# Three expert tiles issued in quarters inside the attention score blocks

## The reference, cut to what matters

```python
x = layernorm(x + L0_attn(x))   # linear attention over L2-normalised Q, K
x = layernorm(x + L0_ffn(x))    # 8 experts, all computed, weighted
x = layernorm(x + L1_attn(x))   # attention between the 16 heads of a token
x = layernorm(x + L1_ffn(x))    # router, top 75% of tokens, gelu(x @ w)
```

```python
# L0_ffn
gate = softmax(x @ gate_w + gate_b)
w = gate * (gate >= 0.1); w = w / sum(w)
out = sum over e of w[:, e] * (x @ expert_w[e] + expert_b[e])     # e = 0..7
# L1_attn
scores = einsum('bnhd,bngd->bnhg', q, k) / 8     # 16 x 16 per token
attn = softmax(scores)
out = einsum('bnhg,bngd->bnhd', attn, v)
```

## Time and profile before

| | |
|---|---|
| median of three runs | 1433.84 us |
| the profiled execution | 1434.45 us, span 1432.6 us |
| PE busy | 84% of the span |
| DVE busy | 64% |
| ACT busy | 51% |
| POOL busy | 40% |
| mean granted TensorE clock | 0.855 of full speed |

### The profile page before, as it was taken

How to read it: one execution, slowest core, us unless ns; L and a number is a source line. 1 busy time by engine, 2 the same in 40 slices (tenths; PEclk the granted TensorE clock), 3 DMA queues, 4 the chain that set the end, 5 groups by cost and what they waited for, 6 DMA issues and landing times.

```text
span 1432.6 us, 31148 instructions
## 1 busy us (share of the span) xinstructions
PE 1202.3 (84%) x12264; PEld 760.1 (53%) x12264; DVE 915.9 (64%) x2113; ACT 733.3 (51%) x1156; POOL 570.2 (40%) x887
## 2 busy tenths in 40 slices
PE   6689899997999899988999899988999898784443
PEld 3444456654665556654665556654665545442442
DVE  3534666587677866587677866587677776464534
ACT  3222465347554765357554675357454675356423
POOL 3125326425424525435424525435524515331312
PEclk8579998899879988899879987899879987787566
DMA  5000090205411190206410290207420290209220
GB/s 177 15 1 15 30 161 4 75 15 148 60 32 45 70 152 3 75 16 148 60 46 31 86 136 2 75 16 154 54 60 2 79 128 2 59 16 168 24 60 30
DMA packets 93145, 90.64 MB, mean 63 GB/s; under 512 B 7110, under 2 KB 81864, under 8 KB 92744
## 3 DMA queue, kind: packets, MB, share of 16 engines
q1 hardware_dynamic: 81736, 76.06, 26.8%
q0 software_dynamic: 2560, 8.39, 1.7%
q10 hardware_dynamic: 8704, 4.20, 1.1%
HBM read 46.68 MB, written 41.94 MB: 62 GB/s over the span
## 4 chain that ended last, share of the span: by engine, by line
PE 53%; DVE 18%; POOL 7%; issue 7%; DMA 6%; ACT 6%; SPq 2%; ACTq 1%; POOLq 0%; DVEq 0%
PE bank L1512 50%; DVE keys L1296 3%; POOL rs L521 2%; DVE x L1201 2%; DVE gelu L1298 2%; DVE stats L1060 2%; ACT x L793 1%; PE bank L1522 1%; DMA scratch_qkv<-part 1%; DMA scratch_qkv<-stage 1%; DMA bt<-scratch_o 1%; DVE ct L1030 1%; DMA scratch_o<-stage 1%; POOL stage L572 1%; DMA ct<-scratch_qkv 1%
## 5 line engine op out<-in xcount | busy, mean ns | idle before, releaser
L1512 PE MATMUL bank<-we,at 128*128 128x512 f16 x1536 | 365.5, 399 | 0.0
L1512 PEld LDWEIGHTS bank<-we,at 128*128 128x128 f16 x1536 | 154.0, 102 | 191.9 <-issue 36.4
L536 POOL TENSOR_TENSOR part<-part 128x512 f32<-128x512 f32 x64 | 83.0, 1297 | 353.8 <-ACTq L819 353.8
L671 ACT ACTIVATE part<-bank,wexp 128x256 f32<-128x256 f32 x256 | 105.2, 471 | 185.7 <-PE bank L1512 124.2
L1201 DVE SCALAR_TENSOR_TENSOR x<-bank,wexp,x 128x256 f32<-128x256 f32 x256 | 122.9, 480 | 81.0 <-PE bank L1512 75.0
L1512 PE MATMUL bank<-bt,wqkv 128*128 128x512 f16 x576 | 139.7, 385 | 15.6 <-DVE stage L1030 12.9
L793 ACT ACTIVATE x<-x,nm,rs 128x256 f32<-128x256 f32 x192 | 104.6, 593 | 92.5 <-POOL nm L524 91.2
L517 POOL TENSOR_SCALAR nm<-mv 128x2 f32<-128x2 f32 x128 | 32.3, 252 | 254.0 <-DVE mv L1065 248.5
L1030 DVE TENSOR_TENSOR stage<-bank,stage 128x512 f16<-128x512 f32 x112 | 75.6, 686 | 85.3 <-ACT stage L671 85.0
L1512 PE MATMUL bank<-keys,blockdiag 128*128 128x16 f16 x3072 | 96.6, 193 | 24.3 <-DMA keys<-scratch_qkv 18.5
L1512 PEld LDWEIGHTS bank<-keys,blockdiag 128*128 128x128 f16 x3072 | 95.6, 104 | 29.5 <-DMA keys<-scratch_qkv 19.0
(11 more groups left out here) (176 smaller groups left out, 2268.8 us busy)
## 6 DMA issues: line engine op xcount, KB each, us to landing
scratch_qkv<-stage SPq DMA_DIRECT2D x40, 512.0 KB, 3.8
ct<-scratch_qkv SPq DMA_DIRECT2D x128, 128.0 KB, 5.7
x_in<-in_x_dram SPq DMA_DIRECT2D x32, 256.0 KB, 2.7
keys<-scratch_qkv SPq DMA_DIRECT2D x64, 128.0 KB, 5.1
bt<-scratch_o SPq DMA_DIRECT2D x16, 512.0 KB, 3.7
out_dram<-x POOLq DMA_DIRECT2D x32, 256.0 KB, 2.7
scratch_qkv<-part SPq DMA_DIRECT2D x8, 512.0 KB, 8.2
scratch_o<-stage SPq DMA_DIRECT2D x32, 128.0 KB, 3.5
```

The costliest lines, as they stand in the source:

```text
L536: pool.tensor_tensor(part[:, 0:2, :], part[:, 0:2, :], part[:, 2:4, :], ALU.add)\
L671: return act.activation(dst, src, ACT.Copy, scale=scale)
L1512: ins = pe.matmul(dst, lhs, rhs, start=(n == 0), stop=(n == len(terms) - 1))
```

## The change

Tile 0 of the experts stays ahead of the score blocks. Tiles 1, 2 and 3, which were issued whole (tile 1 ahead of block 0, tile 2 behind block 1, tile 3 behind block 3), are issued in quarters inside blocks 0, 1 and 2: behind each 24 narrow products of the block stand the six wide products of one quarter. On ACT and on DVE the emptying of tile 2 moves ahead of block 1's softmax. In the turns without scores (c is None) PE's order stays. The whole diff:

```diff
@@ -871,10 +871,10 @@   (ACT, turn)
                     a_moe(b, 1)
                 if c is not None:
                     b_s(c, 0)
+                if b is not None:
+                    a_moe(b, 2)
+                if c is not None:
                     b_s(c, 1)
-                if b is not None:
-                    a_moe(b, 2)
-                if c is not None:
                     b_pt(c, 0)
                     b_s(c, 2)
                     b_pt(c, 1)
@@ -1635,8 +1637,8 @@   (PE)
-            def a_moe(a, t):
-                for q in range(4):
+            def a_moe(a, t, qs=range(4)):
+                for q in qs:
@@ -1661,7 +1663,8 @@
-            def b_s(b, q):
+            def b_s(b, q, tile=None):
@@ -1673,7 +1676,10 @@
-                ins.then_inc(b_full, 1)
+                    if c == 3:
+                        ins.then_inc(b_full, 1)
+                    if tile is not None:
+                        a_moe(b + 1, tile, (c,))
@@ -1752,19 +1758,18 @@   (PE, turn)
                 if b is not None:
                     a_moe(b, 0)
+                if b is not None and c is None:
                     a_moe(b, 1)
-                if c is not None:
-                    b_s(c, 0)
-                    b_s(c, 1)
-                if b is not None:
                     a_moe(b, 2)
-                if c is not None:
+                    a_moe(b, 3)
+                if c is not None:
+                    beside = (None, None, None) if b is None else (1, 2, 3)
+                    b_s(c, 0, beside[0])
+                    b_s(c, 1, beside[1])
                     b_pt(c, 0)
-                    b_s(c, 2)
+                    b_s(c, 2, beside[2])
                     b_pt(c, 1)
                     b_s(c, 3)
-                if b is not None:
-                    a_moe(b, 3)
                 if c is not None:
                     b_pt(c, 2)
```

More of the change, by code:

```diff
@@ L877, in turn @@
                 if c is not None:
+                    b_s(c, 1)
                     b_pt(c, 0)
```

## The result

The changed kernel took 1454.28 us (median of 4 runs, 1447.62 to 1455.76) against 1432.9 us (median of 4, 1430.16 to 1435.29) for the kernel before: a ratio of 1.0141, 95% interval 1.0104 to 1.0178. It is slower by 21.4 us; 24.0 had been forecast. The profiled execution took 1454.86 us, span 1453.0, which is 20.4 us more span.

A forecast was written before the change was run, and what follows sets the result against it. PE held 53% of the chain of waits, but block 3's end was taken to set O0. Six turns' 21.6 us plus the seventh's 2.4 made 24.0; on 1434.45 that gave 1458.4, stated as 1457.8; range 1446 to 1470.

The forecast's parts named there:

- Full clock for tiles 1 to 3: On PE, tiles 2 and 3 fall from 7.09 and 6.44 to 5.18 us each, 3.2 us less a turn.
- Tile 3 in front of block 3: Tile 3's 5.18 us now precede block 3's end; PE alone would start block 3 at least 1.9 us later.
- The chain behind ACT's copies: From tile 2's copies on ACT over POOL and DVE, block 3 starts at 721.9 and ends 3.5 us later.
- O0 8.5 us behind block 3: The first output product follows block 3's end by 8.5 us, before and after, because ACT's work fills that time.
- Six turns 21.6 us: Six turns with experts and scores lose 3.86 + 5 x 3.54 = 21.6 us.
- The seventh turn 2.4 us: Without a new batch, ACT's copies wait for POOL's sum; block 3 comes at 1198.6 against 1196.17, 2.4 us later.
- Nothing takes it back: Later work of a turn hangs on O0 in PE's order, so no later wait recovers the 24.0 us.
- Changes of kind cost nothing: On PE, 24 switches a turn between narrow and wide products cost zero, bounded by 0 to 0.05 us each.
- PE's time decides: Rival: the 3.2 us PE saves on tiles 2 and 3 comes off every turn, giving 1412; 5 in 100.
- the clock does not hold: Rival: in the mixture each tile costs 1.6 us more, 22 us in all, giving 1480; 8 in 100.
- C: Rival: ACT's order does not bite or narrow products get cheaper; only PE's minimum is left, 13 us, 1447; 10 in 100.
- D: Rival: some wait later in the turn takes the delay back, leaving the time within 0.2%; 2 in 100.

The follow-up runs named there:

- the two faster kernels: Against the kernel before: tiles 1, 2, 3 whole behind blocks 1, 2, 3, tile 0 inside block 0 or whole ahead of it; ratios 0.9915 and 0.9924.
- the fastest order: Against the kernel before: tile 0 in quarters inside block 0, tiles 1, 2, 3 whole behind blocks 1, 2, 3, softmaxes moved ahead; 1421.81 us, ratio 0.9915.

## Why the prediction was right, point by point

- **Full clock for tiles 1 to 3.** Right: the clock was 1.00 and every quarter of the turn took 1.30 us. The gain of 3.2 us a turn on PE is real (PE 19 us less busy) and went into its waits.
- **Tile 3 in front of block 3, at least 1.9 us.** Right in kind, 0.4 small in size: PE's own work gives 30.68 us in the changed kernel for the sum's 30.3. As the only cause, in the kernel with block 1 whole, it gave block 3 at 32.05 with tile 2 at the fallen clock.
- **The chain behind ACT's copies.** This was the term that decided, 721.9 against PE's 720.3. Its length from tile 2's end was 10.63 us for a sum of 10.49, and block 3 came 3.63 us later in this turn for 3.5 forecast. The runs show it by PE's waits at PT1: 5.66 us when tile 3 is taken away, 5.70 when the order alone is put into the kernel before. The wait of 1.6 us came as 0.65 at PT1 and 0.70 at block 3, where I had put it all at block 3.
- **O0 8.5 us behind block 3.** It was 8.19 from block 3's last product (735.25) to O0, and from block 3's first product to O0 11.21 for 11.32 before. Right, and PE was idle for 5.9 of it.
- **Six turns 21.6 us.** 21.8 measured.
- **The seventh turn 2.4 us.** This term was mis-sized: it lost 0.8. The order of links held (the exponential of block 1 at 1208.32, right behind the four copies, and block 3 9.46 us later for 9.45 added up), but V's load was there 16.7 us after tile 0 instead of 18.4, and the whole chain hangs on it in that turn. Why the load was sooner by 1.7 us was not tried. In the other kernels with a tile ahead of the blocks it came at 17.0 to 20.9 us, so one trace cannot size this term.
- **Nothing takes it back.** Nearly: 2.2 us came back in the stretches behind O0. The trace gives no one place for it, between single turns it is from a gain of 0.8 to a loss of 0.9, and it was not followed further.
- **Changes of kind cost nothing.** Right: eight pairs of 24 narrow and six wide took 16.22 us, where 192 narrow and 48 wide apart take 16.25.
- **Rivals.** PE's time decides (1412), and the clock does not hold (1480): both excluded by the traces above. C, that ACT's order does not bite, fell with the wait of 0.65 for PT0's bank and block 3 at 32.03 instead of 30.3; D with the ratio.
- **The price of the low clock.** What the Trainium skill ("TensorE: Matmul & The Clock Gate", section "Terms") puts on it, the time spent in it times the share of pulses held back, had given the 1412 of rival A. PE's busy time fell by 19 us where seven times 3.2 are 22, so the price is near for PE's work, and it was no forecast of the end.

## What to carry to other kernels

Cheaper work on the busiest engine is worth nothing where a chain over the other engines sets its next step. Before moving work in front of a block, ask what starts at that block's end, how long that chain is, and what the moved work was lying beside; here the two faster kernels start the chain earlier, and whether the blocks are filled could not be told in their time. Where undoing one edit shows no change, undo a second with it: the larger of two causes on parallel paths hides the other.

## What the runs showed of the hardware that was not expected

A block of 96 narrow products alone behind a mixed block (2.95 us) let the clock fall in one kernel and not in another. With block 1 whole and tile 0 ahead, tile 2 behind it took 6.87 us at a mean clock of 0.75, in each of the first six turns; in the fastest order tile 1 behind it took 5.18 at 1.00, in all seven. Nor does the order settle it: tile 3 of the fastest order took 5.18 us in three of its seven turns and 6.56 to 6.87 in the other four. No run here tells what decides it.

With 24 narrow products between six wide ones a full clock did not fall: the quarters took 1.29 to 1.31 us in all eight traces that have them, but for two of 2.51 us, each behind a wait of PE (2.8 and 6.3 us). The output products took 5.01 us per 192 at a mean clock of 0.93 and 5.27 at 0.50, so narrow products hardly pay for the clock that they lose; the wide ones behind them do.
